# GpSimd left with the index moves, roots on ScalarE and VectorE, and constant tiles prepared one stage early, in a nine-stage transformer kernel

## What is computed

```python
# layer 0, first attention: scores, softmax; then LayerNorm of x + y
h = x + y;  x1 = (h - mean(h)) * rsqrt(var(h) + 1e-5) * gamma + beta
# layer 0, second part (z1 is LayerNorm(x1))
x  = x1 + attention(z1, wq, wk, wv, wo, bo)        # 16 heads of 8, causal
h  = layernorm(x, ln2_scale, ln2_shift)
scores = h @ gate_w                                 # 8 experts
top2 = top_k(scores, 2);  probs = softmax(top2)
x  = x + sum_over_two_experts(probs * (silu(h @ w1[e]) * (h @ w2[e])) @ w3[e])
# layer 1: attention with relative positions, 16 heads of 8
x  = LayerNorm(x);  q, k, v = x @ Wq, x @ Wk, x @ Wv;  r = positions @ Wr
att = softmax(((q + u) k^T + shift((q + v) r^T)) / sqrt(8));  x = LayerNorm(x + att v)
# layer 1, feed-forward of rank 32 with GELU, then LayerNorm
```

## Time and profile before

| | before |
|---|---|
| median of 3 runs | 1982.19 us |
| lowest, highest run | 1959.62, 1989.26 us |
| profiled execution | 1965.66 us |
| its span | 1963.9 us |
| mean granted clock of TensorE | 0.858 of full speed |
| busy share PE, DVE, ACT, POOL | 69%, 60%, 51%, 23% |

### The profile page before, as it was taken

One profiled execution on the slowest core, in us unless ns is written; L12 is line 12 of the kernel. 1 busy time (PEld: TensorE's weight loads), 2 busy tenths in 40 slices (PEclk: granted clock), 3 DMA queues, 4 the chain that ended last, 5 costly groups with the idle time before them and its releaser, 6 DMA issues. The chain is left out here.

```text
span 1963.9 us, 48778 instructions
## 1 busy us (share of the span) xinstructions
PE 1356.6 (69%) x18587; PEld 905.4 (46%) x18775; DVE 1171.8 (60%) x3060; ACT 997.9 (51%) x1988; POOL 449.1 (23%) x756
## 2 busy tenths in 40 slices
PE   6636177777745288745248788787888879888657
PEld 3213044444434277622126555565555556555423
DVE  6943477777345223256317676676767667677636
ACT  4424046666611033223147676676767667776333
POOL 5433235555437600087000000000000000000123
PEclk8867579999955589966679999999999999999868
DMA  8439412222031166548799999999999999999422
GB/s 309 171 103 279 103 43 61 69 62 66 21 101 41 43 179 198 160 136 268 203 339 343 370 377 370 379 379 372 384 378 369 368 379 389 379 377 373 136 66 59
DMA packets 174670, 451.83 MB, mean 230 GB/s; under 512 B 41584, under 2 KB 133776, under 8 KB 157360
## 3 DMA queue, kind: packets, MB, share of 16 engines
q1 hardware_dynamic: 130736, 237.53, 36.7%
q10 hardware_dynamic: 31200, 180.04, 23.3%
q0 software_dynamic: 12512, 31.21, 6.0%
HBM read 222.59 MB, written 225.84 MB: 228 GB/s over the span
## 5 line engine op out<-in xcount | busy, mean ns | idle before, releaser
L2574 DVE CUSTOM_DVE_ANT_0 r_shifted<-r_ps_ac,r_shifted 128x512 f32<-128x512 f32 x512 | 352.0, 688 | 264.1 <-PE r_ps_ac L2449 116.7
L2540 ACT ACTIVATE r_probs<-r_ps_keys 128x512 f32<-128x512 f32 x512 | 309.9, 606 | 215.6 <-PE r_ps_keys L2456 189.4
L2519 ACT ACTIVATE r_wide<-r_ps_wide 128x512 f32<-128x512 f32 (+1 forms) x576 | 330.3, 592 | 84.8 <-PE r_ps_wide L2440 84.6
L2456 PE MATMUL r_ps_keys<-r_ident,r_shifted 128*128 128x128 f32 x2048 | 322.1, 281 | 70.8 <-DMA r_k<-stack 24.4
L2456 PEld LDWEIGHTS r_ps_keys<-r_ident,r_shifted 128*128 128x128 f32 x2048 | 264.1, 145 | 62.9 <-issue 21.5
L2440 PE MATMUL r_ps_wide<-r_r,r_qv 128*32 128x96 bf16 (+12 forms) x6144 | 234.8, 253 | 67.7 <-issue 49.9
L2582 DVE TENSOR_SCALAR r_shifted<-r_shifted,r_mx 128x512 f32<-128x512 f32 x512 | 249.3, 487 | 18.3
L926 ACT ACTIVATE c_probs<-c_ps_keys 128x512 f32<-128x512 f32 (+1 forms) x384 | 174.3, 531 | 140.6 <-PE c_ps_keys L852 140.4
L1135 POOL MEMSET n_zeros<- 128x4 f32 x1 | 0.1, 101 | 906.7 <-POOLq L2275 906.7
L2440 PEld LDWEIGHTS r_ps_wide<-r_r,r_qv 128*32 128x32 bf16 x6144 | 103.6, 97 | 164.5 <-issue 163.7
L2469 PE MATMUL r_ps_out<-r_probs,r_v 128*9 128x128 f32 x4096 | 142.4, 274 | 21.1 <-issue 20.4
(11 more groups left out here) (249 smaller groups left out, 1948.8 us busy)
## 6 DMA issues: line engine op xcount, KB each, us to landing
skew<-r_wide ACTq DMA_DIRECT2D x64, 2224.0 KB, 13.6
r_shifted<-skew SPq DMA_DIRECT2D x64, 2160.0 KB, 13.6
by_expert<-a_blank ACTq DMA_DIRECT2D x4, 4352.0 KB
e_w<-in_L_ffn_w_dram SPq DMA_DIRECT2D x117, 128.0 KB, 2.4
c_qk<-qk_stacks POOLq DMA_DIRECT2D x64, 192.0 KB, 3.7
stack<-d_part SPq DMA_DIRECT2D x96, 128.0 KB
qk_stacks<-b_part SPq DMA_DIRECT2D x48, 128.0 KB, 3.5
qk_stacks<-b_part POOLq DMA_DIRECT2D x48, 128.0 KB, 3.7
```

The lines of the kernel that those rows point to most:

```text
L2456: last = pe.transpose(ps_keys[u % 2][:, j * P:(j + 1) * P], shifted[:, s, W * u + j * P:W * u + (j + 1) * P], ident[:, :])
L2519: act.activation(wide[:, s, c, lo:hi], ps_wide[bk % BANKS][:, 0:hi - lo], ACT.Copy).then_inc(wide_sb, 1)
L2540: act.activation(probs[:, h % 2, :, b * P:(b + 1) * P], ps_keys[u % 2][:, :].rearrange("p (j i) -> p j i", j=NT), ACT.Exp, scale=SCALE).th ...
L2574: dve.tensor_tensor_reduce(out=shifted[:, s, W * u:W * u + L], in0=ps_ac[u % 2][:, :], in1=shifted[:, s, W * u:W * u + L], scale=1.0, scal ...
```

## The change

- **Causal attention (b, c).** The ring `qk` now lives through stages b and c. GpSimd sets rows 32 to 63 of each half to minus one in stage b (two MEMSETs of 32x4096 as f32, behind its first MEMSETs and ahead of its wait for the positions). In stage c VectorE's two MEMSETs and GpSimd's wait for them are gone.
- **LayerNorm statistics in m and d.** A class `RootNorm` takes the place of `Norm`: ACT takes the square root (`root`, with eps as its bias), VectorE the reciprocal (`invert`); both tiles have two slots.
- **Merge (m).** The bias enters through PE: ahead of the four matmuls of `project(n)` stands one of a single row, `ones[0:1]` against `bo`, 128x512. The residual is added from `x`. VectorE makes the negated, scaled mean in `scale_rows(n)` right behind `merge(n)`. The sigmoids of all sequences are two instructions at the end. GpSimd keeps the pattern constants and the 64 indirect DMAs.
- **Combine (d).** GpSimd's list has the gathers alone; ACT's `root(n + 1)` stands between the first and the second of its three copies of n.
- **Expert blocks (e).** GpSimd clears `r`, `qu`, `k` and `qv` in this stage, and SP loads `ident` and the positions' stack into `r` behind the loads of block 8.
- **Relative attention (r).** The clearing, the two loads and the waits for them are gone.

The diff, cut to its core:

```diff
+class RootNorm:
+    def root(self, act, n):
+        act.wait_ge(self.var_ready, n + 1)
+        act.activation(self.std[:, n % 2, :], self.mv[:, n % 2, :, 1], ACT.Sqrt, bias=self.eps[:, 0:1])\
+            .then_inc(self.std_ready, 1)
+
+    def invert(self, dve, n):
+        dve.wait_ge(self.std_ready, n + 1)
+        dve.reciprocal(self.rstd[:, n % 2, :], self.std[:, n % 2, :]).then_inc(self.rstd_ready, 1)
+        dve.wait_ge(self.rstd_ready, n + 1)
...
 def phase_project
+            if causal_qk is not None:
+                pool.wait_ge(ones_set, n_set)
+                for half in range(2):
+                    rows = causal_qk[P // 2 * half + P // 4:P // 2 * half + P // 2, :, 1, :, :]
+                    pool.memset(rows.rearrange("r s p t -> r s (p t)").bitcast(F32), MINUS_ONES)\
+                        .then_inc(rows_set, 1)
...
 def phase_causal
-            pool.wait_ge(preset, 2)
             for s in range(FIRST):
                 load(pool, s, s)
...
-            for half in range(2):
-                dve.memset(qk[ROWS * half + 32:ROWS * half + ROWS, :, 1, :, :].rearrange("r s p t -> r s (p t)"), -1.0)\
-                    .then_inc(preset, 1)
...
 def phase_route, ACT
+            norm.root(act, 0)
             act.wait_ge(route_loaded, 16 * 5)
             for n in range(NB):
                 normalized(n)
+                if n + 1 < NB:
+                    norm.root(act, n + 1)
                 turned(n)
-                if n >= 1:
-                    shares(n - 1)
-            shares(NB - 1)
+            shares()
...
 def phase_route, PE, in project(n)
+                pe.matmul(ps[n % SETS][:, :], ones[0:1, :], bo[0:1, :].unsqueeze(1).broadcast_to([1, NT, P]),
+                          start=True, stop=False, skip_group_check=True)
...
 def phase_route, VectorE
+            def scale_rows(n):
+                if n >= 2:
+                    dve.wait_ge(z_ready, n - 1)
+                norm.invert(dve, n)
+                dve.scalar_tensor_tensor(out=minus[:, n, :], in0=norm.mv[:, n % 2, :, 0], scalar=-1.0,
+                                         in1=norm.rstd[:, n % 2, :], op0=ALU.mult, op1=ALU.mult)\
+                    .then_inc(minus_ready, 1)
...
                 merge(n)
+                scale_rows(n)
...
 def phase_blocks, SP and GpSimd
                 load_tokens(b)
                 load_weights(b)
+                if b == 2 * SLOTS:
+                    sp.dma_start(rel_ident[:, :], ident_in).then_inc(positions_loaded, 16)
+                    sp.wait_ge(cleared, 1)
+                    for s in range(2):
+                        sp.dma_start(rel_r[P // 2 * s:P // 2 * s + SK, :, :, :],
+                                     rel_r_in.rearrange("r (o g h) t -> g r o h t", g=2, h=G)[s])\
+                            .then_inc(positions_loaded, 16)
...
+            for i, tile in enumerate((rel_r, qu_tile, k_tile, qv_tile)):
+                if i >= 1:
+                    pool.wait_ge(cleared, i)
+                pool.memset(tile[:, :, :, :].rearrange("p s h t -> p (s h t)").bitcast(F32), 0.0).then_inc(cleared, 1)
...
 def phase_combine, GpSimd and ACT
-            for n in range(NB):
-                norm.root(pool, n + 1)
-                if n + 2 < NB:
-                    gather(n + 2)
+            for n in range(2, NB):
+                gather(n)
...
                 for c in range(NC):
+                    if c == 1 and n + 1 < NB:
+                        norm.root(act, n + 1)
...
 def phase_relative
-            sp.wait_ge(pad_set, 1)
             load_queries(0, 0)
             load_queries(0, 1)
-            sp.wait_ge(pad_set, 2)
-            sp.dma_start(ident[:, :], ident_in).then_inc(consts, 16)
...
-            for stack in (qv, r, qu, k):
-                dve.memset(stack[:, :, :, :].rearrange("p s h t -> p (s h t)").bitcast(F32), 0.0)\
-                    .then_inc(pad_set, 1)
```

More of the change, by code:

```diff
@@ L1 @@
+import struct
 from contextlib import ExitStack
@@ L137, in apply, with __init__, constants, moments @@
                                      ALU.subtract, ALU.mult)
+        return last
+class RootNorm:
+    def __init__(self, ctx, nc, sems, name):
+        self.stats = ctx.enter_context(nc.sbuf_tensor(name + "_stats", [P, NT, 6], F32))
+        self.mv = ctx.enter_context(nc.sbuf_tensor(name + "_mv", [P, 2, NT, 2], F32))
+        self.std = ctx.enter_context(nc.sbuf_tensor(name + "_std", [P, 2, NT], F32))
+        self.rstd = ctx.enter_context(nc.sbuf_tensor(name + "_rstd", [P, 2, NT], F32))
+        self.eps = ctx.enter_context(nc.sbuf_tensor(name + "_eps", [P, 1], F32))
+        self.eps_set = sems.new(name + "_eps_set")
+        self.stats_ready = sems.new(name + "_stats_ready")
+        self.var_ready = sems.new(name + "_var_ready")
+        self.std_ready = sems.new(name + "_std_ready")
+        self.rstd_ready = sems.new(name + "_rstd_ready")
+    def constants(self, pool):
+        pool.memset(self.eps[:, :], EPS).then_inc(self.eps_set, 1)
+    def moments(self, dve, x, n):
+        for t in range(NT):
+            last = dve.bn_stats(self.stats[:, t, :], x[:, t, :])
+        last.then_inc(self.stats_ready, 1)
+        dve.wait_ge(self.stats_ready, n + 1)
+        for t in range(NT):
+            last = dve.bn_aggr(self.mv[:, n % 2, t, :], self.stats[:, t, :])
+        last.then_inc(self.var_ready, 1)
+    def root(self, act, n):
[6 more added lines that the diff above has]
+        dve.wait_ge(self.rstd_ready, n + 1)
+    def apply(self, dve, out, x, n):
+        for t in range(NT):
+            last = dve.tensor_scalar(out[:, t, :], x[:, t, :], self.mv[:, n % 2, t, 0:1],
+                                     self.rstd[:, n % 2, t:t + 1], ALU.subtract, ALU.mult)
         return last
@@ L460, in phase_project @@
 def phase_project(nc, sems, z_in, scale, shift, w_in, biases, tables, ident_in, stacks_out, v9_out, name,
-                  positions=None):
+                  positions=None, causal_qk=None):
     NC = len(w_in) - 1
@@ L580, in _ @@
             pool.sem_inc(pool_slots, 2)
+            if causal_qk is not None:
[4 more added lines that the diff above has]
+                        .then_inc(rows_set, 1)
+                    pool.wait_ge(rows_set, half + 1)
             if positions is not None:
@@ L1970, in store_terms @@
                 term_stores(act, n, NC - 1, act_stored[n % 2])
+            act.wait_ge(norm.eps_set, 1)
+            norm.root(act, 0)
             act.wait_ge(consts, n_const)
@@ L2631, in program @@
             sems = Semaphores(nc, sems)
[L2632 removed]
+            phase_combine(nc, sems, (base, pos, pr), expert_out, [rel_wqT, rel_wqT, rel_wkT, rel_wvT],
+                          [u_bias, v_bias, None], [TERMS_Q, TERMS_Q, TERMS_K], ident, x2, stacks[2:5], v9[1])
         sems = Semaphores(nc, sems)
[L2634 to L2635 removed]
```

164 lines of the change are left out of this document (64 added, 100 removed).

## The result

| | before | changed |
|---|---|---|
| median | 1971.28 us (14 runs) | 1987.60 us (14 runs) |
| lowest, highest | 1959.62, 1989.26 us | 1976.06, 1995.34 us |
| ratio | | 1.0058 (95%: 1.0035 to 1.0082) |
| profiled execution, its span | 1965.66, 1963.9 us | 1995.34, 1993.8 us |

The changed kernel is 0.6% slower, where I had forecast 1932 us and a range that ended at 1957. The two profiled executions stand 29.9 us apart in their spans and overstate the difference of the medians (16.3 us) by some 14 us.

The account below looks back on a forecast made before the run. No engine was busy over 69%, so each stage was read for its own limit (GpSimd in m, SP in e). Terms 14 + 11 - 8 + 9 + 16 = 42 us less, from 1973.9 to 1932 us; range 1908 to 1957.

Parts of the forecast that it names:

- c: Stage c start: GpSimd loads at once without VectorE's clearing, PE starts near 220 instead of 234.4; 14 us less.
- m: Stage m: GpSimd keeps only scatters, the last starting at 666.4 instead of 678.9; 11 us less, bounds 5 to 14.
- e: Stage e: the positions' load delays block 9's tokens and SP issues three more loads; 8 us more, bounds 1.5 to 12.6.
- d: Stage d: roots leave GpSimd, shortening its rounds of gathers; 9 us less, bounds 3 to 14.
- r: Stage r start: clearing and loads already done, PE begins at 965.5 instead of 981.4; 16 us less, bounds 7 to 17.
- GpSimd keeps 64 scatters of 0.96 + 0.30: Stage m: scatters follow one another every 1.26 us without a gap, 81 us in all.
- A root costs GpSimd ... 1.2 us: Stage d: seven roots on GpSimd stand in the way of the last sequence; removing them saves 8.6 us.
- From then on the stage ... shifts as a whole: Stage r after its start is bound by its DMAs, so the 16 us gained at the start carries through.
- The one-row matmul: Stage m, bias on PE: priced at the full 1.91 us of a 128x512 matmul; if depth counted, total gain some 44.
- A: Rival: moved work meets full resources, DMA in stage d (3 us gain), positions' load in e (12.6 lost); 1943 us, chance 0.22.
- B: Rival: PE's or VectorE's round in m outgrows GpSimd's (gain 5), r's issue wait stays (gain 7); 1947 us, chance 0.12.
- C: Rival: VectorE's work in stage m stretches each of 64 scatters by 1.45 us, 93 us more; 2036 us, chance 0.03.

Follow-up runs that it names:

- without late signals: The changed kernel itself, nothing altered, rerun on a third chip where waiting engines heard of finished work promptly: 1943.35 us, ratio 0.9850.
- The shorter chain: Kernel with positions in stage m and 1.8 us stops in d, plus stage m's turned copy before the root and bias matmul before the turn: 1935.66 us, ratio 0.9790.

## Why the prediction was wrong, point by point

In us against the profile of before; the last column is the changed kernel without late signals.

| term | forecast | first result | without late signals |
|---|---|---|---|
| c | -14 | -8.4 | -8.3 |
| m | -11 | +4.5 | -9.8 |
| e | +8 | +11.0 | +9.4 |
| d | -9 | +17.5 | -12.1 |
| r | -16 | +6.0 | -3.6 |
| sum | -42 | +30.6 | -24.4 |

*Stages m and d, the steps that failed.* The steps were "GpSimd keeps 64 scatters of 0.96 + 0.30", 81 us in all, and "A root costs GpSimd ... 1.2 us", of which "seven stand in the way". In the first result the scatters took 95.5 us (580.5 to 676.0), since GpSimd stood and waited for late indices, and stage m became 4.5 us longer where I had 11 less; stage d became 17.5 us longer where I had 9 less. Without late signals both steps hold: the scatters run from 580.3 to 661.8 us, 81.5 us, and stage d gains 12 us, with rounds of 11.7 us on average (I had 11.4 to 11.8). What failed is the assumption under both, that a signal takes the same time whatever GpSimd does. I had read VectorE's waits for scores in stage m of the kernel before as PE's; four of them reached 1.4 to 3.8 us beyond PE's end, and each ended within 0.3 us of the end of an eight of scatters. PE ends at 607.86; the timeline of the kernel before goes on:

```profile
608.22 0.96 POOL L1387 DMA_INDIRECT by_expert<-m_z,m_pos  x1 [0.30 <-issue]
609.29 0.19 DVE L1528 COPY m_scores<-m_ps_s 128x32 f32<-128x32 f32 x1 [2.34 <-PE m_ps_s L1457]
```

That was a sign, in view, of what a row without a stop might do. The run with stages b and c alone, of the other face, shows what it was worth. VectorE's waits for scores in stage m (us in total, times, longest), first before, then in that run:

```profile
DVE m_scores L1528 <- remote: 7.7, 3, 3.1
```

```profile
DVE m_scores L1535 <- PE m_ps_s L1464: 1.9, 2, 1.0
```

Stage m is of one length in both (141.3 and 141.1 us): in the kernel before GpSimd set the pace, and signals that came late between the others cost nothing. In the changed kernel a round of PE (9.8 us, from 581.38 to 591.21) and eight scatters (10.1 us) are nearly equal, and such signals cost time.

*Stage c, a term mis-sized.* The last constant took 6 us to land where I took 2 to 5 and a landing of GpSimd's loads as the upper end. 10.1 us at the first matmul in place of 14, and 8.3 to 9.6 at the end.

*Stage e, right in kind, a little small.* The place, the single long round and the missing catch-up were as forecast; 9.4 to 11.0 us for 8, within its bounds. The loss that I had at 6.5 us was 9.7 (12.9 less 3.2), the issues 1.9 for 1.5. The reason I gave for the size, the order within SP's queue, is not needed: from GpSimd's queue the load cost the same.

*Stage r, half right.* The start gained what was forecast (position scores 15.2 us earlier, first shifted load 15.5). "From then on the stage ... shifts as a whole" failed. Over all profiles stage r takes 875.9 us on average with the prepared start (17, from 865.6 to 889.2) and 882.7 without (3, from 878.3 to 886.4): 7 us of 15 are left. With three profiles on one side and that spread the size is uncertain, and what gives it back was not tried. Beside stage c this is why the gain stays under the forecast even where no signal is late.

*The one-row matmul.* Its price was right. Two passes take 2.07 us against 1.91 at full depth, so a single row makes it no cheaper. The Trainium skill ("TensorE: Matmul & The Clock Gate", LDWEIGHTS (loading the stationary operand)) says of the weight load that its time goes by columns and not by depth; the trace agrees, and shows it for the matmul as a whole. But it stood on the chain from one turn to the next, where I had compared busy times only. The shorter chain got it off.

*The rivals.* A is wrong where signals are on time: stage d gained 12 us, not 3; that 1943.35 is also A's number is luck. B foresaw gaps between the eights of scatters, for another reason. C looked at the index moves, held up by VectorE: of 64 scatters none took over 1.4 us, of 64 gathers two took over 2 us in the first result and five without late signals, as five did before. It was all others that were held up beside them. None of the three has the mechanism that decided.

*The sum.* Where no signal is late, the change brings 30 us of 1975.3 by the ratio (18 to 41), and 1943.35 lies in my range; by the table the change is worth 24 of the 42 us. Where signals are late it costs 0.4 to 0.6%. I had no case for two faces of one kernel, and the chance of 0.03 for slower was too small for that.

## What to carry to other kernels

When GpSimd is cleared of everything but indirect transfers, try a stop of about 2 us between the eights and look whether all other engines' waits become shorter. In stage d that cost 7 us where signals are on time and saved 22 where they are late. Move a large load to a stage whose DMA share is low *and* whose other loads are not waited for round by round; another queue does not help. And time a candidate on more than one chip before it is called slower: the variant with the stops of 1.8 us and the positions in stage m is faster by 1.7% and by 1.5% in the two faces, the change as it was made by -0.6% and 1.5%.

## What the hardware showed that I had not expected

- Beside gathers issued 1.25 us apart for 62 us, signals between VectorE, ACT and PE came up to 8 us late, even from VectorE to itself. The Trainium skill ("SBUF — State Buffer", Who interferes with whom) knows one contention between engines, the port that VectorE shares with GpSimd. By that page ACT and PE have no part in it; here they waited too, and no run shows for what.
- It is not a matter of the transfers' bandwidth: between 883 and 898 us, while nearly all stood still, the transfers moved 52 GB/s, against 273 in stage d before.
- After eight gathers a MEMSET of 1.8 us was enough where signals are late (stage d 130.0 to 130.6 us in three runs), one of 0.9 us (153.6) and one of 0.1 us (153.0) were not.
- The changed kernel had this in its first result and on the fourth chip, and not on the third. The second chip had it with four kernels and did not have it with four others ten minutes later.
